# Five strided instructions of one metaformer layer walk pixel by pixel within a channel instead of channel by channel within a pixel

## What is computed

```python
x = x + conv_ref(ln_c(x))           # L0_conv: a mixer with a convolution along channels, two attentions
t = to_tokens(x)                    # (128, 81, 256): one row of 256 channels per image and pixel
t = t + ffn_ref(ln_t(t))            # top 2 of 8 experts, 256 -> 512 -> 256, exact gelu
x = from_tokens(t)

def ln_c(v):                        # over the channels of one pixel
    return (v - v.mean(1)) / sqrt(v.var(1) + 1e-6)

# the first piece of conv_ref: for each pixel a 9-tap convolution along the channels
k  = x.reshape(bs, c, hw).transpose(0, 2, 1)
k1 = conv_1d(k, se_key_w, groups=hw) + se_key_b[None, :, None]
```

## Time and profile before

| | |
|---|---|
| median of 3 runs | 1658.89 us (1657.28 to 1659.47) |
| the profiled execution | 1662.11 us, of which its span is 1660.4 us |
| PE busy | 1251.2 us, 75% of the span |
| DVE busy | 1101.1 us, 66% |
| ACT busy | 720.6 us, 43% |
| POOL busy | 535.8 us, 32% |
| moved by DMA | 267.87 MB |

### The profile page before, as it was taken

The page is one execution under the profiler, slowest core; times in us unless marked ns, Lnnn a source line. Parts: engine busy times, 40 slices in busy tenths (PEclk is TensorE's granted clock), DMA queues, the critical chain, the costliest instruction groups (busy, mean ns, idle before and its releaser), DMA issues.

```text
span 1660.4 us, 36623 instructions
## 1 busy us (share of the span) xinstructions
PE 1251.2 (75%) x9504; PEld 1024.6 (62%) x9505; DVE 1101.1 (66%) x2637; ACT 720.6 (43%) x1741; POOL 535.8 (32%) x497
## 2 busy tenths in 40 slices
PE   0197879896999999997556522999999999999200
PEld 0187778892565565557545512888888888888100
DVE  7796456564778777775676672666666666666493
ACT  0293233333555555554667641333333333333350
POOL 0163111110111111110467774444454545544100
PEclk9997788887999999995555555999999999999655
DMA  8536787869878888861233444222222333222576
GB/s 314 136 91 183 243 285 282 323 240 244 192 175 184 182 185 197 197 147 53 96 131 134 140 155 130 86 86 89 89 89 84 88 92 93 90 90 70 230 284 256
DMA packets 239768, 267.87 MB, mean 161 GB/s; under 512 B 119696, under 2 KB 211988, under 8 KB 235818
## 3 DMA queue, kind: packets, MB, share of 16 engines
q1 hardware_dynamic: 219413, 214.20, 44.6%
q0 software_dynamic: 20320, 53.28, 9.6%
HBM read 158.69 MB, written 116.19 MB: 166 GB/s over the span
## 4 chain that ended last, share of the span: by engine, by line
PE 59%; DVE 11%; ACT 8%; DMA 8%; SPq 4%; issue 4%; POOL 4%; DVEq 0%; POOLq 0%; ACTq 0%
PE ps L803 15%; PE ps L788 14%; POOL rows_d L1621 4%; PE ps L596 3%; PE ps L613 3%; PE ps L562 3%; DMA u_d<-in_zstrings 3%; PE ps L627 2%; PE ps L772 2%; DVE big L1361 2%; PE ps L674 2%; PE ps L629 2%; DVE pool_ L1353 2%; PE ps L618 2%; ACT aux L1493 2%
## 5 line engine op out<-in xcount | busy, mean ns | idle before, releaser
L1630 POOL DMA_INDIRECT y_d<-pool_,to_s x176 | 254.8, 1448 | 278.7 <-DVE pool_ L1321 242.5
L803 PE MATMUL ps<-pool_,aux 128*128 x2112 | 248.7, 274 | 6.0 <-DVE aux L1313 3.4
L788 PE MATMUL ps<-aux,pool_ 128*128 128x256 f16 x2112 | 247.5, 274 | 0.6 <-ACT aux L1543 0.3
L803 PEld LDWEIGHTS ps<-pool_,aux 128*128 128x128 f16 x2112 | 199.8, 98 | 49.9 <-issue 25.3
L788 PEld LDWEIGHTS ps<-aux,pool_ 128*128 x2112 | 206.4, 98 | 25.9 <-issue 1.2
L1543 ACT ACTIVATE aux<-ps,b_s 128x256 f32<-128x256 f32 x352 | 138.3, 475 | 162.5 <-DVE aux L1313 162.0
L1621 POOL DMA_INDIRECT rows_d<-aux,idx_s x162 | 159.0, 982 | 103.4 <-DVE idx_s L1223 54.3
L1610 POOL DMA_DIRECT2D pool_<-v_d x64 | 47.9, 753 | 338.6 <-PE ps L682 323.8
L1321 DVE SCALAR_TENSOR_TENSOR pool_<-ps,pool_ 128x512 f32<-128x512 f32 x88 | 60.9, 692 | 140.6 <-PE ps L803 140.6
L1535 ACT ACTIVATE aux<-ps 128x512 f16<-128x512 f32 x88 | 52.5, 597 | 188.8 <-PE ps L772 188.8
L1313 DVE TENSOR_TENSOR aux<-aux 128x1024 f16<-128x1024 f32 x88 | 107.9, 1226 | 3.1
(11 more groups left out here) (209 smaller groups left out, 2691.2 us busy)
## 6 DMA issues: line engine op xcount, KB each, us to landing
pool_<-rows_d SPq DMA_DIRECT2D x88, 258.0 KB
pool_<-y_d SPq DMA_DIRECT2D x18, 1152.0 KB, 8.5
big<-in_x SPq DMA_DIRECT2D x2, 5184.0 KB, 21.0
xn_d<-big SPq DMA_DIRECT2D x16, 648.0 KB, 5.4
aux<-in_x SPq DMA_DIRECT2D x64, 162.0 KB, 2.9
v_d<-aux SPq DMA_DIRECT2D x64, 162.0 KB, 2.6
ks_d<-big SPq DMA_DIRECT2D x16, 648.0 KB, 3.8
pool_<-v_d POOLq DMA_DIRECT2D x64, 162.0 KB, 3.3
```

The source lines that it names most:

```text
L788: last = nc.tensor.matmul(o, w_s[:, a, bass.ds(e * (4 * PIECE) + (k * HID + j * 128), 128)], xh_s[:, par, b, k * SLOTS:(k + 1) * SLOTS], s ...
L803: last = nc.tensor.matmul(ps[:, 6 + par, s * C:(s + 1) * C], hh_s[:, par, a, j, s * 128:(s + 1) * 128], w_s[:, b, bass.ds(e * (4 * PIECE) ...
L1630: nc.gpsimd.indirect_dma_start(out=y_d[:, :], out_offset=bass.IndirectOffsetOnAxis(ap=to_s[:, par, k:k + 1], axis=0), in_=yo_s[:, par, k, ...
```

## The change

Five instructions copy or add the same elements as before, between the same buffers, and wait for the same semaphores; the dimensions of its access patterns are put in another order. Before, the walk was pixel by pixel and within a pixel channel by channel (or, in `tokens`, image by image). Now it is channel by channel (image by image), and within that over the 3 pixels of the turn or group (2 in `k1_out`, whose third pixel has an instruction of its own as before). In the big buffer an instruction so meets runs of 3 (or 2) neighbours of 4 bytes. Its other operand is walked in the same order: PSUM with a step of 1024 bytes inside a run (`k1_out`, `rows`), `got_s` in SBUF with 1024 bytes (`finish`, read), `xs_s` with 512 bytes (`tokens`, written) and `xp_s` with 1024 bytes (`xn_back`, read). No instruction is added, removed or moved to another place of an engine's order.

```diff
--- before.py
+++ after.py
@@ -274,7 +274,7 @@
         x1_s = big[:, :].rearrange("p (h t) -> p h t", h=HALVES)
 
 
-        x1_pixels = big[:, :].rearrange("p (h b n) -> p h n b", h=HALVES, b=BS)
+        x1_pixels = big[:, :].rearrange("p (h b n) -> p h b n", h=HALVES, b=BS)
         x1_turned = by_pixel(big)
 
         W_IN = 16 * 20
@@ -911,9 +911,9 @@
                 dve.wait_ge(S["k1_c"], i + 1 + CREDIT)
                 for k in range(0, PIX, 2):
                     n = min(2, PIX - k)
-                    ins = nc.vector.tensor_tensor(by_pixel(pool_)[:, bass.ds(i * PIX + k, n), :],
-                                                  ps[:, 4 + 2 * par + k // 2, 0:n * C].rearrange("p (k c) -> p k c", k=n),
-                                                  kb_s[:, bass.ds(i * PIX + k, n)].unsqueeze(2).to_broadcast([128, n, C]),
+                    ins = nc.vector.tensor_tensor(pool_.rearrange("b (c p) -> b c p", p=HW)[:, :, bass.ds(i * PIX + k, n)],
+                                                  ps[:, 4 + 2 * par + k // 2, 0:n * C].rearrange("p (k c) -> p c k", k=n),
+                                                  kb_s[:, bass.ds(i * PIX + k, n)].unsqueeze(1).to_broadcast([128, C, n]),
                                                   ALU.add)
                 ins.then_inc(S["k1_ev"], 1)
 
@@ -1356,9 +1356,10 @@
 
             def finish(r):
                 slot, at = r // SUBS % SLOTS_Y, r % SUBS * SUBS
-                x1 = x1_turned[:, r * SUBS:(r + 1) * SUBS, :]
+                x1 = x1_turned[:, r * SUBS:(r + 1) * SUBS, :].rearrange("b s c -> b c s")
                 dve.wait_ge(S["mix_c"], r + 1)
-                nc.vector.tensor_tensor(x1, x1, got_s[:, slot, 0, at:at + SUBS, :], ALU.add).then_inc(S["fin_c"], 1)
+                nc.vector.tensor_tensor(x1, x1, got_s[:, slot, 0, at:at + SUBS, :].rearrange("b s c -> b c s"),
+                                        ALU.add).then_inc(S["fin_c"], 1)
 
             dve.wait_ge(S["x1t_c"], TURNS)
             combine(0)
@@ -1471,8 +1472,8 @@
 
                 if r > 2:
                     act.wait_ge(S["rl_p"], r - 2 + CREDIT)
-                nc.scalar.activation(xs_s[r % 3].rearrange("p h (s b) -> p h s b", s=SUBS),
-                                     x1_pixels[:, :, r * SUBS:(r + 1) * SUBS, :], ACT.Copy).then_inc(S["xs_c"], 1)
+                nc.scalar.activation(xs_s[r % 3].rearrange("p h (s b) -> p h b s", s=SUBS),
+                                     x1_pixels[:, :, :, r * SUBS:(r + 1) * SUBS], ACT.Copy).then_inc(S["xs_c"], 1)
 
             def deviations(r):
 
@@ -1494,9 +1495,9 @@
                                          ACT.Identity, bias=bs_s[:, p, 9:10], scale=bs_s[:, p, 8:9])
                 nc.scalar.activation(xf_s[:, r % RING, :, C + 1:WIDE], token_s[:, r * SUBS:(r + 1) * SUBS].unsqueeze(2),
                                      ACT.Copy).then_inc(S["xft_c"], 1)
-                nc.scalar.activation(x1_turned[:, r * SUBS:(r + 1) * SUBS, :],
+                nc.scalar.activation(x1_turned[:, r * SUBS:(r + 1) * SUBS, :].rearrange("b s c -> b c s"),
                                      ps[:, 2 * slot:2 * slot + 2, :].rearrange("p b n -> p (b n)")[:, 0:SUBS * C]
-                                     .rearrange("p (s c) -> p s c", s=SUBS), ACT.Copy).then_inc(S["x1t_c"], 1)
+                                     .rearrange("p (s c) -> p c s", s=SUBS), ACT.Copy).then_inc(S["x1t_c"], 1)
 
             def high_piece(n, slot, come):
 
@@ -1582,7 +1583,8 @@
 
                 pool.wait_ge(S["xp_c"], i + 1)
                 settle()
-                nc.gpsimd.tensor_copy(by_pixel(big)[:, bass.ds(i * PIX, PIX), :], xp_s[:, par]).then_inc(S["xb_c"], 1)
+                nc.gpsimd.tensor_copy(big.rearrange("b (c p) -> b c p", p=HW)[:, :, bass.ds(i * PIX, PIX)],
+                                      xp_s[:, par].rearrange("b k c -> b c k")).then_inc(S["xb_c"], 1)
 
             with pool.Fori(0, PIX_TURNS // 2) as i:
                 for par in range(2):
```

## The result

The changed kernel takes **1647.41 us** in the median of 4 runs (1643.96 to 1648.76), the kernel before 1658.85 us beside it. The ratio is 0.9929, 95% interval 0.9912 to 0.9947: 11.4 us or 0.7% faster. The profiled execution is the one of 1648.76 us, its span 1647.0.

The account below looks back on a forecast made before the run. ACT paces the pixel stage, POOL's scatters the routing, a full DVE the last stage. `rows` 3.5 plus `k1_out` 0.6, 4.1 us off the median 1658.89, gave 1654.8 us; range 1651.5 to 1663.

Parts of the forecast that it names:

- rows: Routing, L1497: from 1530 to 940 ns; six on the chain start POOL's scatter run 3.5 us earlier.
- and as much off its end: Routing: POOL's scatter run, starting 3.5 us earlier, would also end 3.5 us earlier, its length unchanged.
- tokens: Routing, L1474: read in runs, written 512 bytes apart; 1530 ns, zero gain, bounds 940 and 2309.
- finish: Last stage, L1361: far read of `got_s` keeps 1512 ns, zero gain; bounds 1066 and 2081.
- k1_out: Pixel stage, L914: from 1056 to some 850 ns; 0.6 us at the stage's end, bounds 0 and 1.2.
- xn_back: Pixel stage, L1585 on POOL: 1556 ns, between 1088 and 2024; covered by POOL's idle time, nothing on the path.
- that PSUM pays: Rival: PSUM pays at 1024 bytes or runs of 3 save nothing; `rows`, `k1_out` keep their prices, 1659 us; chance 0.13.
- Dearer steps of 1024 bytes: Rival: 1024-byte SBUF steps cost more than 324; `finish` at 2081 ns adds 15.4 us, 1670.2; chance 0.11.
- POOL's outgrown cover: Rival: in the pixel stage `xn_back` exceeds 2.2 us and delays ACT; at 2492 ns 7.9 us, 1662.7; chance 0.09.
- "cheap" rival: Rival: far steps returning to the same places are cheap; `finish` 1066 ns saves 12 us, `tokens` 1.2; 1641.6 us; chance 0.07.

Follow-up runs that it names:

- e4: Changed kernel with `finish` cut along channels: three additions per load, each over 9 pixels by 85 or 86 channels; 1659.1 us.
- e2: Changed kernel with `finish` put back to pixel by pixel, the other four instructions as changed; 1657.3 us, ratio 0.9999.
- e1: Kernel before with the edit of `finish` alone; 1645.93 us, ratio 0.9926.
- e3: Changed kernel with one unused float after each row of 256 in `got_s`, so `finish` reads 1028 bytes apart; 1651.8 us.
- e6: Changed kernel with the layout of the copy in `tokens` turned, so its writes are 1024 bytes apart instead of 512; 1643.84 us.

## Why the prediction was wrong

1. **`rows`.** 940 ns were forecast, 947 measured; POOL's run began 3.4 us earlier, as worked out. (30 ns over 64 runs are 0.47 a run and not 0.48, which makes 937.) Right up to there. The step that failed is "and as much off its end": the run was taken as 144 scatters "at their own rate". That rate depends on what DVE does beside them, and the new phase cost 4.5 us in held scatters (7.09 - 2.58), of which 0.8 us came back from the rest of the run.
2. **`tokens`.** 1530 forecast, 1557 measured, no gain. Right.
3. **`finish`: the step that made the prediction wrong.** It said "By the earlier trace rows a far read alone costs what it cost before: 1512, zero gain". It costs 1040. The nearest row walked over 9 places (L1193), and a walk over 9 does pay, as e4 shows; three places cost 0.1 us over the 943 of neighbours. The mechanism stood in the text as a rival with 0.07, and its price of 1066 was right. What I did not weigh is that the one row against it differed in the number of places, the very thing the rival was about. One row at 9 is no evidence on 3; the rival deserved several times its chance, with the range down to it. That the kernel became faster at all, as forecast, is luck: the two terms that were to bring it, `rows` and `k1_out`, brought nothing that e2 can measure, and the gain came from a term that stood at nothing.
4. **`k1_out`.** Some 850 ns forecast, 715 measured: nearer to its floor of 629 than to the middle. The chain's last two fell from 1.52 us to 1.22, and the transfer of k1 starts at 141.56 instead of 142.72:

```profile
140.33 1.22 DVE pool_ L914 x2
141.55 0.02 issue
141.56 8.86 DMA k_d<-pool_
```

   But e1, where `k1_out` is unchanged, has it at 141.83, and the kernels with the new walk between 140.58 and 142.42. Nothing can be told of a gain here.
5. **`xn_back`.** 1556 forecast, 1072 measured: POOL reads three places 1024 bytes apart at the price of neighbours (1088, an estimate by elements from the earlier trace rows). The cover made the miss harmless. The estimate from the "GPSIMD Engine Reference" of the Trainium skill, section 7, had been 1856 ns; the measurement decides against it here.

The rivals: that PSUM pays fell with 947 and 715 ns. The Trainium skill's "PSUM — Partial Sum Buffer", section Specifications (TRN2), says of matmuls that a non-contiguous pattern slows them significantly; these two evictions take 0.13 and 0.09 us more than the plain prices estimated for them (817 and 629), far from their old ones. Dearer steps of 1024 bytes fell with e3 and e6, POOL's outgrown cover with 1072 ns. The "cheap" rival came true for `finish` (its 12 us, measured 12.4), not for `tokens`, where the walk is on the written side; its 1641.6 us were too low by what the routing gave back and that part. With 3.5 + 0.6 us of my sum lost and 12.4 found, the sum would have been 1646.5.

The stage that gained has the bound that it had. DVE runs without a break from its first `combine` at 1562.40 us to 1620.3, 27 turns of 2.14 us. ACT waits for the loads, but that is not what DVE waits for, and it was so before (the second row):

```profile
L1564 ACT ACTIVATE pool_<-pool_,posw_s 128x256 f32<-128x256 f32 x81 | 33.3, 495 | 36.6 <-DMA pool_<-y_d 36.6
```

```profile
L1563 ACT ACTIVATE pool_<-pool_,posw_s 128x256 f32<-128x256 f32 x81 | 33.3, 494 | 42.1 <-DMA pool_<-y_d 42.1
```

What is new is that the loads hardly wait for slots: ACT begins on the last at 1605.04 us instead of 1611.41, seven loads after 1566.53, so one comes each 5.5 us. DVE takes 6.4 us for the three turns of a load. As an estimate from these, a `finish` that is faster by another 0.3 us would meet the loads; no run tried it.

## What to carry to other kernels

Where an elementwise instruction must step far in SBUF, keep the write in runs, put the step on the read and let it go round few places. Over three places that was nearly free here on DVE and on POOL; ACT paid a third of the full price over two, three were not tried there, and a far write over three places was tried on ACT alone, where it paid in full. Count the places before pricing a walk by a row of the trace, since three and four are different prices. An engine that seems to run "at its own rate" may be held by its neighbour: compare the mean duration of its unchanged instructions before and after, and look at what the neighbour has under way when the long ones begin. And an instruction that waits on another engine costs what is queued behind it: one step later in the order was worth more here than any of the walks but one.

## What the runs showed of the hardware

- DVE, second operand, 1024 or 1028 bytes between places that the walk returns to: 1.35 ns an element over three places (1036 to 1041 ns for 768), 1.89 to 2.01 over four, five and nine. No run shows why the jump lies between three and four.
- ACT: far reads over two places 1199 ns for 768, over four 1509 to 1516, in runs of three 997; far writes 1555 to 1557, over three places too.
- POOL: a far read over three places, written in runs of 3, costs as much as neighbours: 1072 ns, against 1088 by an estimate from a copy of 324.
- A scatter on POOL is held from 0.12 us after its start to the end of a DVE instruction with two inputs from SBUF that began before it, by up to 0.63 us in the changed kernel. One that begins after the scatter makes it longer by 0.08 us at most in the 18 kernels, and reductions, and statistics from PSUM, hold it not at all.
- PE's weight load of 128 columns takes 227 ns from weights 12 bytes apart, as from neighbours.
